# Return matmuls two pairs behind instead of one, and 97 blocks a half instead of 100, in a fused spectral-filter and mixture-of-experts kernel

## The reference

```
x = x + conv(layernorm_over_channels(x))   # 64 -> 16 channels, 2-D FFT, gain per frequency, inverse FFT, 16 -> 64
t = x as 8192 tokens of 64 channels
u = layernorm(t)
p = softmax(u @ gate_w + gate_b)           # 16 experts, the top 2 of each token kept and normalised
t = t + sum over its 2 experts of p_e * ((silu(u @ w1[e]) * (u @ w2[e])) @ w3[e])    # hidden 128
```

## Time and profile before

| | |
|---|---|
| time of 3 runs | 378.09 us median, 378.05 to 382.96 |
| the profiled execution | 375.32 us |
| its span, first to last instruction | 373.5 us |
| mean granted TensorE clock | 0.840 |
| busy: TensorE matmul, VectorE, ScalarE, GpSimd | 277.1, 244.9, 212.4, 99.6 us |

### The profile page before, as it was taken

How to read it: one execution, slowest core, us unless ns; L and a number is a source line. 1 busy time by engine, 2 the same in 40 slices (tenths; PEclk the granted TensorE clock), 3 DMA queues, 4 the chain that set the end, 5 groups by cost and what they waited for, 6 DMA issues and landing times. The chain is left out here.

```text
span 373.5 us, 8436 instructions
## 1 busy us (share of the span) xinstructions
PE 277.1 (74%) x2886; PEld 229.5 (61%) x2886; DVE 244.9 (66%) x664; ACT 212.4 (57%) x486; POOL 99.6 (27%) x96
## 2 busy tenths in 40 slices
PE   3969666967372862699999988886778777790985
PEld 3837345855152532588888877775667667780764
DVE  1973674498899979498977766445554555521895
ACT  3868844662073753487878764454554555540674
POOL 2016264340044532222223240051112210003770
PEclk9958985555855588599999999998999998895799
DMA  8996333330011113214344434362333432122551
GB/s 228 343 251 227 122 119 121 123 123 7 0 55 70 51 62 104 91 50 126 114 125 115 118 107 106 93 178 78 93 89 88 129 101 59 40 64 71 153 176 61
DMA packets 44254, 41.39 MB, mean 111 GB/s; under 512 B 27564, under 2 KB 39070, under 8 KB 43574
## 3 DMA queue, kind: packets, MB, share of 16 engines
q1 hardware_dynamic: 40886, 30.35, 27.8%
q0 software_dynamic: 3168, 10.50, 8.7%
q10 hardware_dynamic: 160, 0.01, 0.0%
HBM read 20.71 MB, written 20.14 MB: 109 GB/s over the span
## 5 line engine op out<-in xcount | busy, mean ns | idle before, releaser
L1326 DVE SCALAR_TENSOR_TENSOR power<-banks,fold 128x500 f32<-128x500 f32 x50 | 33.8, 677 | 62.9 <-ACT fold L624 57.0
L1413 POOL DMA_INDIRECT sorted_x<-xs,addr x32 | 34.6, 1081 | 100.4 <-ACT xs L591 98.9
L1419 POOL DMA_INDIRECT xs<-sorted_y,back x32 | 32.3, 1010 | 107.4 <-DMA sorted_y<-filt 57.6
L975 PE MATMUL banks<-w_all,power 128*125 x400 | 55.4, 284 | 0.5
L975 PEld LDWEIGHTS banks<-w_all,power 128*125 128x125 f32 x400 | 49.5, 195 | 4.2 <-issue 2.3
L591 ACT CAST xs<-banks 128x384 f16<-128x384 f32 x64 | 27.1, 439 | 37.5 <-PE banks L871 37.5
L1317 DVE COPY work<-w_all 128x512 uint16 (+1 forms) x200 | 40.0, 263 | 8.8 <-issue 8.7
L624 ACT ACTIVATE fold<-banks 128x500 f32<-128x500 f32 x50 | 29.9, 597 | 19.9 <-PE banks L963 19.3
L963 PE MATMUL banks<-shared,work 128*128 128x125 f16 x300 | 40.9, 223 | 0.0
L962 PE MATMUL banks<-shared,work 128*128 128x125 f16 x300 | 40.9, 225 | 0.0
L638 ACT CAST xs<-xs 64x320 f16<-64x320 f32 x64 | 29.2, 456 | 20.4 <-DVE xs L1330 14.8
(11 more groups left out here) (192 smaller groups left out, 578.4 us busy)
## 6 DMA issues: line engine op xcount, KB each, us to landing
sorted_x<-zeros SPq DMA_DIRECT2D x2, 3125.0 KB
w_raw<-sorted_x SPq DMA_DIRECT2D x24, 250.0 KB
sorted_y<-filt SPq DMA_DIRECT2D x26, 125.0 KB
sorted_y<-enh SPq DMA_DIRECT2D x24, 125.0 KB
w_raw<-in_L_ffn_w SPq DMA_DIRECT2D x5, 512.0 KB, 16.0
xs<-in_x SPq DMA_DIRECT2D x8, 256.0 KB, 5.2
out<-cen_sq SPq DMA_DIRECT2D x8, 256.0 KB, 2.7
shared<-in_t_fwd SPq DMA_DIRECT2D x1, 1024.0 KB, 7.8
```

The costliest lines, as they stand in the source:

```text
L975: last = nc.tensor.matmul(y_bank(q)[0:BW, b * C:(b + 1) * C], hid[:, q % RING, b * BW:(b + 1) * BW], of_expert(experts[(q % NQ % 2) * QUAD ...
L1326: nc.vector.scalar_tensor_tensor(hid[:, q % RING, 0:QW], bank[2 + q % 2][:, 0:QW], HSCALE / WSCALE, gated[:, q % 2, 0:QW], ALU.mult, ALU.m ...
L1413: nc.gpsimd.indirect_dma_start(out=sorted_x[k].rearrange("(g s) c -> g (s c)", s=GRP), out_offset=bass.IndirectOffsetOnAxis(ap=addr[:, k, ...
L1419: nc.gpsimd.indirect_dma_start(out=yl[m % YL_RING].rearrange("g s c -> g (s c)"), out_offset=None, in_=sorted_y[k].rearrange("(g s) c -> g ...
```

## The change

`BACK_LAG` becomes 2 and `RESULT_LAG` 3: in the step of pair m, TensorE issues the return matmuls of pair m-2, and ScalarE copies sums out one pair later. `SLOT_BLOCKS` is 97 and no longer rounded up. `NQ` is still 25 and there are still 13 octets, but the last quad of each half (q = 24 and q = 49) has one block of 125 rows; every instruction that works on a quad takes its size from `blocks_in(q)` or from the two helpers for octets. The last octet's load brings 25 partitions instead of 100, and its five transposes are 25 wide, each starting at an even column. The fill with zeros still covers 100 blocks.

```diff
-SLOT_BLOCKS = -(-((HT * TGROUPS + E * (GBLK - 1)) // GBLK) // QUAD) * QUAD
-NQ = SLOT_BLOCKS // QUAD
+SLOT_BLOCKS = (HT * TGROUPS + E * (GBLK - 1)) // GBLK
+NQ = -(-SLOT_BLOCKS // QUAD)
...
-RET_START, RET_STEPS, BACK_LAG = 4, 18, 1
-RESULT_LAG = 2
+RET_START, RET_STEPS, BACK_LAG = 4, 18, 2
+RESULT_LAG = 3
...
+        def blocks_in(q):
+
+            return min(QUAD, SLOT_BLOCKS - QUAD * (q % NQ))
+
+        def quads_in(o):
+
+            return -(-blocks_of(o) // QUAD)
+
+        def quad_groups(o):
+
+            return min(QG, blocks_of(o) * GBLK)
...
             def store_y(q):
                 k, i = q // NQ, q % NQ
                 sp.wait_ge(y_done, q + 1)
-                sp.dma_start(sorted_y[k][i * QW:(i + 1) * QW, :].rearrange("(b p) c -> p b c", p=BW),
-                             ys[q % YS_RING][0:BW, :].rearrange("p (b c) -> p b c", b=QUAD)).then_inc(y_stored[q % YS_RING], 16)
+                sp.dma_start(sorted_y[k][i * QW:i * QW + blocks_in(q) * BW, :].rearrange("(b p) c -> p b c", p=BW),
+                             ys[q % YS_RING][0:BW, 0:blocks_in(q) * C].rearrange("p (b c) -> p b c", c=C)).then_inc(y_stored[q % YS_RING], 16)
...
-                nc.scalar.activation(gated[:, q % 2, 0:QW], bank[q % 2][:, 0:QW], ACT.Silu, scale=1.0 / WSCALE).then_inc(silu_done, 1)
+                w = blocks_in(q) * BW
+                nc.scalar.activation(gated[:, q % 2, 0:w], bank[q % 2][:, 0:w], ACT.Silu, scale=1.0 / WSCALE).then_inc(silu_done, 1)
...
-                for r in range(blocks_of(o) // QUAD * GRP):
-                    last = nc.tensor.transpose(bank[XT_BANK].bitcast(F16)[:, r * QG:(r + 1) * QG], xg[:, n % XG_RING, r * P:(r + 1) * P], ident16[0:QG, 0:QG])
+                w = quad_groups(o)
+                apart = w + w % 2
+                for r in range(quads_in(o) * GRP):
+                    last = nc.tensor.transpose(bank[XT_BANK].bitcast(F16)[:, r * apart:r * apart + w], xg[0:w, n % XG_RING, r * P:(r + 1) * P], ident16[0:w, 0:w])
...
-                    for b in range(QUAD):
+                    for b in range(blocks_in(q)):
                         dst = bank[first_bank + q % 2][:, b * BW:(b + 1) * BW]
...
-                for b in range(QUAD):
+                for b in range(blocks_in(q)):
                     last = nc.tensor.matmul(y_bank(q)[0:BW, b * C:(b + 1) * C], hid[:, q % RING, b * BW:(b + 1) * BW],
```

More of the change, by code:

```diff
@@ L273, in build @@
         block_end = sb("block_end", [E, HALVES])
-        past = sb("past", [E, HALVES, SLOT_BLOCKS], F16)
+        past = sb("past", [E, HALVES, NQ * QUAD], F16)
         owner = sb("owner", [1, HALVES, OCTETS * OCT], I32)
@@ L430, in load @@
                 k, o = n // OCTETS, n % OCTETS
-                w = blocks_of(o) // QUAD
+                w, groups_in = quads_in(o), quad_groups(o)
                 if o == 0:
@@ L436, in load @@
                     sp.wait_ge(xt_ps, n - XG_RING + 1)
[L437 to L438 removed]
+                sp.dma_start(xg[0:groups_in, n % XG_RING, 0:w * GRP * P].rearrange("p (h n) -> p h n", n=GRP * P),
+                             sorted_x[k][o * OROWS:o * OROWS + w * groups_in * GRP, :].rearrange("(h p s) c -> p h (s c)", p=groups_in, s=GRP)).then_inc(in_xg[n % XG_RING], 16)
             def store_y(q):
@@ L449, in _ @@
                 k, o = n // OCTETS, n % OCTETS
-                for h in range(blocks_of(o) // QUAD):
+                for h in range(quads_in(o)):
                     store_y(NQ * k + 2 * o + h)
@@ L609, in tokens_out @@
             def tokens_out(n):
-                w = blocks_of(n % OCTETS) // QUAD
+                w, groups_in = quads_in(n % OCTETS), quad_groups(n % OCTETS)
                 act.wait_ge(xt_ps, n + 1)
@@ L613, in tokens_out @@
                     act.wait_ge(h2_done, quads_through(n - 2))
-                turned = bank[XT_BANK].bitcast(F16)[:, 0:w * QW].rearrange("p (h s b g) -> p h b g s", s=GRP, b=QUAD, g=GBLK)
-                kept_at = xt[:, n % 2, 0:w * QW].rearrange("p (h b g s) -> p h b g s", s=GRP, b=QUAD, g=GBLK)
+                apart = groups_in + groups_in % 2
+                turned = bank[XT_BANK].bitcast(F16)[:, 0:w * GRP * apart].rearrange("p (h s n) -> p h s n", h=w, s=GRP)
+                turned = turned[:, :, :, 0:groups_in].rearrange("p h s (b g) -> p h b g s", g=GBLK)
+                kept_at = xt[:, n % 2, 0:w * groups_in * GRP].rearrange("p (h b g s) -> p h b g s", h=w, s=GRP, g=GBLK)
                 for h in range(w):
@@ L629, in y_out @@
                     act.wait_ge(y_stored[q % YS_RING], 16 * (q // YS_RING))
-                nc.scalar.activation(ys[q % YS_RING][0:BW, :], y_bank(q)[0:BW, 0:QUAD * C], ACT.Copy, scale=1.0 / (WSCALE * HSCALE * WT_SCALE)).then_inc(y_done, 1)
+                w = blocks_in(q) * C
+                nc.scalar.activation(ys[q % YS_RING][0:BW, 0:w], y_bank(q)[0:BW, 0:w], ACT.Copy, scale=1.0 / (WSCALE * HSCALE * WT_SCALE)).then_inc(y_done, 1)
             def high_part(m):
@@ L855, in owners_for @@
                 pe.wait_ge(past_done, k + 1)
-                nc.tensor.matmul(bank[MISC_BANK][0:HT, 2 * P:2 * P + SLOT_BLOCKS], ones[0:E, 0:HT], past[:, k, :], start=True, stop=True).then_inc(owner_ps, 1)
+                nc.tensor.matmul(bank[MISC_BANK][0:HT, 2 * P:2 * P + SLOT_BLOCKS], ones[0:E, 0:HT], past[:, k, 0:SLOT_BLOCKS], start=True, stop=True).then_inc(owner_ps, 1)
             def sort_pair(n, a):
@@ L1325, in product @@
                     dve.wait_ge(y_ps, q - RING + 1)
-                nc.vector.scalar_tensor_tensor(hid[:, q % RING, 0:QW], bank[2 + q % 2][:, 0:QW], HSCALE / WSCALE, gated[:, q % 2, 0:QW], ALU.mult, ALU.mult).then_inc(hid_done, 1)
+                w = blocks_in(q) * BW
+                nc.vector.scalar_tensor_tensor(hid[:, q % RING, 0:w], bank[2 + q % 2][:, 0:w], HSCALE / WSCALE, gated[:, q % 2, 0:w], ALU.mult, ALU.mult).then_inc(hid_done, 1)
             def weigh(m):
```

4 lines of the change are left out of this document (2 added, 2 removed).

## The result

The changed kernel takes 359.15 us (358.75 to 360.27, 4 runs) against 379.61 us of the kernel before (378.05 to 382.96, 4 runs, one more than was known ahead): ratio 0.949, 95% interval 0.945 to 0.953. The forecast was 357, range 352 to 366.5. The profiled execution took 359.35, its span is 357.5 us.

The account below looks back on a forecast made before the run. The prediction took a latency ring, with no engine full, to bound the kernel. Terms 17.0 + 1.4 + 2.5 = 20.9 us off the median of 378.09 gave 357.2, rounded to 357; range 352 to 366.5.

Parts of the forecast that it names:

- First edit: Second half's interleaved stretch: return matmuls one pair later end TensorE's wait for the low part; 17.0 us less, bounds 12 and 20.
- the 19.2 of the sum by rows: Quad 31's product to quad 47's: TensorE's own work sums to 56.5 us against 75.68, 19.2 less before deductions.
- the ring: Same stretch: product, weights fetched, weigh, low part, return matmuls, up, gate, product follow without overlap, 4.73 us per quad.
- The two kinds of step: TensorE's loop steps after the first edit: 3.22 us without an octet's transposes, 4.14 us with them.
- I take TensorE as the bound, but the margin is thin: Loop after the first edit: TensorE's mean step of 3.68 us stays just above ScalarE and VectorE's shared ring.
- its own work sets the pace: Loop after the first edit: TensorE goes through up, down, transposes and return without stopping, at 3.22 and 4.14 us a step.
- Rival A: Loop: ScalarE and VectorE become the bound, work not overlapping; the first edit gives 8.3 us, total 366; chance 0.2.
- Clock: Loop: one drop of TensorE's granted clock after the first edit, about 1.2 us left ungained.
- Waits of ScalarE for the buffers, and the results' lag: Loop: ScalarE's high-part wait for return matmuls of pair m-3 can't bind; moving results by one pair adds no new wait.
- Second edit, forecast 1.4 at the border: Quad 24, one block instead of four: up 0.67 us less and down 0.69 less, 1.36 in all.
- those stand behind up(24) and are not shortened: Border: TensorE's 1.15 us wait before quad 25 is for ScalarE's copies, which come behind up(24) and keep their length.
- Second edit, forecast 2.5 at the end: Quad 49 to the last gathers: one block shortens up, down, y_out, transposes and store; 2.5 us, bounds 1.5 and 3.3.

Follow-up runs that it names:

- the lags alone: The changed kernel with 100 blocks a half again, return lag 2 and result lag 3 kept; ratios 0.930 and 0.935 to the kernel before on two chips.
- Experiment 2: The changed kernel's 97 blocks with the lags of the kernel before (BACK_LAG 1, RESULT_LAG 2); ratio 0.999 to the kernel before.
- experiment 4: The kernel before with the first f32 matmul of each return inside the loop issued twice; ratio 0.995 to the kernel before.
- experiment 1: The changed kernel with 100 blocks a half again, both lags kept; median 354.65 us against 379.52 for the kernel before, ratio 0.930.
- experiment 10: The changed kernel with 100 blocks and both lags kept, run again on another chip; median 355.62 us, ratio 0.935 to the kernel before.
- experiment 7: The changed kernel with 100 blocks, return lag 2, but RESULT_LAG left at 2; ratio 0.944 to the kernel before.
- experiment 3: The changed kernel (97 blocks) with the first f32 matmul of each return inside the loop issued twice; ratio 0.942 to the kernel before.
- experiment 9: The changed kernel itself, unaltered, run again on another chip beside the kernel before; median 355.25 us, ratio 0.935.
- the last job: One chip: the changed kernel and its 100-block version, each without and with filler matmuls, beside the kernel before; all four ratios 0.935.

## Why the prediction was right, point by point

**First edit, forecast 17.0 with bounds 12 and 20: the cut works as described, and brings more than forecast.** The loop lost 17.4 us in the changed kernel's profile, 19.4 and 18.8 in the two of the lags alone (75.68 less 56.32 and 56.86). With no fall of the clock in those two, the 19.2 of the sum by rows is met within 0.4. Experiment 2 shows that the wait stays without this edit, experiment 4 that TensorE had room ahead of it.

By the medians the lags alone bring 24.9 us in experiment 1 and 24.6 in experiment 10, and experiment 7 has 21.8: all above the upper bound of 20. Of this 1.8 come at the end, from 13.39 to 11.63 (below). The rest is argued: the forecast took its loop from an execution of 375.32 us, which lies 3.2 to 4.9 below the medians that the kernel before had beside the experiments. The three profiles with the old lag (the kernel before, experiments 4 and 2) took 375.32, 377.63 and 380.15 us, with loops of 75.68, 77.25 and 79.91 and mean clocks there of 0.93, 0.92 and 0.85, so nearly all that sets them apart lies in the loop. A usual execution of the kernel before then spends more time at the lower clock in the ring than the one that was read. So it is partly luck that the sum came out near in the first comparison: the first edit brings more than its term and the second, in the medians, next to nothing.

The two kinds of step were each mis-sized, in opposite directions: 2.89 for 3.22, because the small gaps behind up and L1005, which I took from a TensorE that kept stopping, close when it doesn't; and 4.24 for 4.14, because the gap of the register load grew from 0.42 to a mean of 0.76. Together 0.2 too much.

**"I take TensorE as the bound, but the margin is thin": right for the total, not for most steps.** The loop takes what TensorE's sum says, and TensorE hardly waits in it. But the ring of ScalarE and VectorE takes 6.96 us for two steps where TensorE takes 7.14, its lengths are found in 14 of the 16 steps of experiment 1, and 4.1 us of added work on TensorE (experiment 3) lengthened the loop by 0.9 beside experiment 9 and 2.2 beside experiment 1. What "its own work sets the pace" left out is that two rings are nearly equal, and which of them binds changes along the loop. Rival A, at 366, had these two engines serial in every octet step; they do set most of the steps, but the octet's copies run beside VectorE's work, so its price did not come.

**Clock.** I left 1.2 us for one drop in the loop. The changed kernel had one at 284 to 289 us, after idle times of 0.69 and 1.18 at quad 38; its repeat and the lags alone had none. The Trainium skill (TensorE: Matmul & The Clock Gate, "A second HAM failure mode: psum-queue depth-cycling") says that frequent short idle times between groups of matmuls make the clock swing between its levels. This case agrees with it only in part: three of the four loops at two pairs without further edits had no fall, yet each of the four kept seven idle times of 0.38 to 1.43 us ahead of its transposes.

**Waits of ScalarE for the buffers, and the results' lag: right.** ScalarE waited for the return matmuls only with a lag of three, and then for 2.5 us in all. `RESULT_LAG` made no difference.

**Second edit, forecast 1.4 at the border: the mechanism held for half of it, and the gain does not show in the time.** The step that failed is "those stand behind up(24) and are not shortened". The saving of up(24) was given back to a wait for ScalarE and to the register load within the same step; that of down(24) was real. In the profiles 9 and 10, with a full clock, the stretch is 1.3 shorter, about half of it by down(24); in the one that belongs to the result it was 1.9 longer, under the low clock. In the loop behind it, where the forecast had nothing, 97 blocks lose 0.8 and 0.6 us.

**Second edit, forecast 2.5 at the end: 2.8 measured, more than half of it from the other edit.** The blocks bring 1.25. The rest, 13.39 to 11.63 us, comes with the lags alone: TensorE now runs further ahead of VectorE. The last octet's transposes start 0.68 us ahead of the product of quad 47 (313.77, 314.45), where they came 0.89 behind it (328.86 and 327.97), and the last two quads' matmuls follow that much sooner. For the store I took 0.8 between bounds 0 and 1.5; 0.4 was measured, and 0.85 of waiting for SP stood against it. The prediction's "all that time the queues move 90 GB/s" holds for the middle of the store only: from 335 to 340 us they moved 45, 87, 90, 90 and 70. Its picture of a queue that drains is borne out all the same, by the figures of experiment 9 above. The Trainium skill (DMA: Bandwidth & Descriptors, "Latency and other measured facts") puts the fixed cost of a DMA at about 2 us, by which the shorter store would have given 0. The measured 0.4 lies midway between that and my 0.8, and no store here runs alone, so no run tells the fixed cost from the queue.

**Sum, forecast 20.9: 20.5 by the medians of the first comparison, 25.0 by those of the second** (380.25 and 355.25). The forecast's own range was also added up loosely: 20 + 1.4 + 3.3 and 12 + 1.4 + 1.5 below 378.09 are 353.4 and 363.2, where it has 352.5 and 362.

By the two clean profiles the blocks save 1.3 at the border, 1.25 at the end and 0.4 behind the last store, of 3.9 forecast; but they lose 0.8 in the loop, and 0.7 goes ahead of quad 19's product, where they do not act. What is left is 1.5, the difference of the spans (352.8 and 351.3). So little cannot be told from nothing in the medians: 0.999 for the blocks alone and 0.935 for both kernels in the last job. A usual execution may lose it to the clock as well, but this is only argued. Executions with 97 blocks have the lower mean clock (0.832 to 0.849 over the five runs of 9 that the comparison uses, 0.841 to 0.851 over the six of 10), and in 9 the times follow it, 353.15 us at 0.849 and 357.14 at 0.832; in 10 they do not (356.28 at 0.851, 354.58 at 0.845). Fillers at the two places where profiles had shown the low clock brought nothing. Why the changed kernel is at 0.949 on one chip and at 0.935 on another stays open; the mean clock does not explain it, as an execution of the first comparison took 358.95 us at 0.847.

## What to carry to other kernels

Follow a repeated wait round until it closes: where engines at 50 to 75 per cent wait for each other in one ring, taking the consumer's step from the round before cuts the ring, and the new pace can be read off ahead as the sum of each engine's own groups, start to start. Then look for the second ring at once, since it may be within 3 per cent of the first, and test which one binds with the same kernel plus a little work, nothing else changed. A gain read from one profile holds for that execution; see first where its time lies among the others. And a saving of 1 per cent on TensorE's work can vanish in the spread of its clock and in the difference between chips; compare such edits on one chip, in one job, with more than one profile each, and follow a saving through all later stretches, since a load of registers took part of it back here.

## What the runs showed of the hardware that was not expected

- Around the load of eight registers TensorE's array is idle for 0.38 to 1.03 us in the loop of experiment 1 (up to 1.43 in experiment 9) although the four f32 blocks of down (0.92 us) stand in front of it, and for 0.96 us in the mean without them. Less work in front makes the gap longer: behind down(22) it is 0.45 to 0.47 us in all seven profiles with 100 blocks and the load behind down, and 0.66 to 0.76 in all six with 97, where up(24) has 4 matmuls instead of 16.
- The granted clock at one place of the same kernel differs between executions: 0.69 and 1.00 from 230 to 240 us.
- A store of 125 pieces of 256 bytes takes 4.3 us to land behind other stores, one of 500 such pieces 4.7, while the queues move about 90 GB/s.
